# One GNN kernel: on VectorE, x1 of the row tile before goes ahead of the turned unit

## What is computed

```python
h = maximum(layernorm(x), 0)
support = relu(quantised(h) @ quantised(weight))        # small integers
x1 = x + adj @ quantised(support)                       # layer 0
h = maximum(layernorm(x1), 0)
A = (adj + adj.T) * 0.5 + I ;  d = rowsum(A) ** -0.5    # layer 1
y = adj @ ((d[:, None] * A * d[None, :]) @ h)
out = x1 + y
```

## Time and profile before

| what | value |
|---|---|
| median of 3 runs | 499.73 us (499.46 to 500.01) |
| profiled execution, its own time | 499.41 us |
| its span | 497.5 us |
| TensorE (PE) matmul busy | 482.9 us, 97% |
| VectorE (DVE) busy | 275.2 us, 55% |
| ScalarE (ACT) busy | 136.0 us, 27% |
| GpSimd (POOL) busy | 46.5 us, 9% |
| granted TensorE clock | full in all 40 slices |

### The profile page before, as it was taken

The page is one execution under the profiler, slowest core; times in us unless marked ns, Lnnn a source line. Parts: engine busy times, 40 slices in busy tenths (PEclk is TensorE's granted clock), DMA queues, the critical chain, the costliest instruction groups (busy, mean ns, idle before and its releaser), DMA issues.

```text
span 497.5 us, 6362 instructions
## 1 busy us (share of the span) xinstructions
PE 482.9 (97%) x2390; PEld 236.6 (48%) x2390; DVE 275.2 (55%) x367; ACT 136.0 (27%) x192; POOL 46.5 (9%) x54
## 2 busy tenths in 40 slices
PE   3999998999999999999999999999999999999997
PEld 2755554445554444444444444444444444444446
DVE  6964969989999688785996777340000000000000
ACT  1796634433432343534512122140000000000000
POOL 2322932332200000000000000000000000000000
PEclk9999999999999999999999999999999999999999
DMA  8978996779677233233223231045010000100001
GB/s 296 402 315 191 303 243 130 130 172 208 152 216 288 65 106 124 87 107 104 86 89 122 88 123 42 1 134 224 22 42 21 21 21 21 42 21 21 22 21 43
DMA packets 54731, 60.56 MB, mean 122 GB/s; under 512 B 37688, under 2 KB 37944, under 8 KB 54712
## 3 DMA queue, kind: packets, MB, share of 16 engines
q1 hardware_dynamic: 54704, 60.30, 40.5%
q10 hardware_dynamic: 8, 0.00, 0.0%
HBM read 42.99 MB, written 8.39 MB: 103 GB/s over the span
## 4 chain that ended last, share of the span: by engine, by line
PE 84%; DVE 7%; DMA 3%; SPq 2%; ACT 1%; issue 1%; POOL 0%; ACTq 0%; DVEq 0%; POOLq 0%
PE ps_a L1163 31%; PE ps_p L1062 13%; PE ps_p L1126 7%; PE ps_a L1126 7%; PE ps_b L1126 7%; PE ps_m L1126 4%; PE ps_h L1126 4%; DMA feat<-in_x 2%; DVE at L720 2%; PE ps_b L1013 1%; PE ps_m L1062 1%; PE ps_h L1062 1%; DVE at L715 1%; DVE small L900 1%; PE ps_b L1179 1%
## 5 line engine op out<-in xcount | busy, mean ns | idle before, releaser
L1062 PE MATMUL ps_p<-small,at 128*128 128x512 f16 x448 | 100.0, 379 | 2.0 <-DVE feat L840 2.0
L982 DVE SCALAR_TENSOR_TENSOR feat<-ps_a,feat 128x512 f32<-128x512 f32 (+1 forms) x16 | 10.8, 676 | 148.7 <-PE ps_a L1163 144.2
L1163 PE MATMUL ps_a<-small,at 128*128 128x512 f16 x360 | 80.2, 379 | 0.0
L1163 PE MATMUL ps_a<-a_in,at 128*128 128x512 f16 x360 | 80.2, 379 | 0.0
L1062 PEld LDWEIGHTS ps_p<-small,at 128*128 128x128 f16 x448 | 43.6, 98 | 51.5 <-DVE feat L840 2.5
L551 ACT ACTIVATE split<-a_in 128x1024 f16<-128x1024 f32 x30 | 31.7, 1057 | 101.5 <-PE ps_p L1126 90.0
L1163 PEld LDWEIGHTS ps_a<-a_in,at 128*128 (+1 forms) x360 | 35.2, 98 | 42.5
L1163 PEld LDWEIGHTS ps_a<-small,at 128*128 (+1 forms) x360 | 35.2, 98 | 42.5
L896 DVE TENSOR_TENSOR split<-a_in,split 128x1024 f16<-128x1024 f32 x30 | 36.7, 1224 | 33.7 <-ACT split L551 33.7
L1126 PE MATMUL ps_p<-feat,split 128*128 (+1 forms) x180 | 43.9, 379 | 0.5 <-DVE small L900 0.5
L1126 PE MATMUL ps_a<-feat,split 128*128 (+1 forms) x180 | 43.8, 379 | 0.0
(11 more groups left out here) (179 smaller groups left out, 432.5 us busy)
## 6 DMA issues: line engine op xcount, KB each, us to landing
a_in<-in_adj SPq DMA_DIRECT2D x46, 512.0 KB, 3.9
at<-in_adj SPq DMA_DIRECT2D x16, 512.0 KB, 10.0
out<-feat SPq DMA_DIRECT2D x31, 256.0 KB, 4.2
feat<-in_x SPq DMA_DIRECT2D x8, 512.0 KB, 10.8
feat<-out SPq DMA_DIRECT2D x4, 1024.0 KB, 9.3
at<-in_L_gnn_weight SPq DMA_DIRECT2D x2, 512.0 KB, 3.8
at<-at SPq DMA_TRANSPOSE x34, 3.3
split<-in_adj SPq DMA_DIRECT2D x1, 512.0 KB, 16.2
```

The costliest lines, as they stand in the source:

```text
L982: nc.vector.scalar_tensor_tensor(out, products, 1.0 / (SA * SZ), out, ALU.mult, ALU.add).then_inc(y_out, 1)
L1062: last = nc.tensor.matmul(l0_bank(r), at_block(r, lo, j), small[:, j * D:(j + 1) * D], start=(j == 0 and lo == 0), stop=(j == T - 1 and lo ...
L1163: last = nc.tensor.matmul(BANK[n], at_block(t, lo, j), z_part(j, z_lo), start=(j == 0 and lo + z_lo == 0), stop=(j == T - 1 and lo == 1))
```

## The change

VectorE does `x1_tile(r - 1)` before the turned unit of row tile r instead of after it, for every r from 1 to 13. No instruction is added, taken away or changed; TensorE, ScalarE, GpSimd and SP keep their order.

```diff
             for r in range(1, 14):
                 now = TURNS[r]
+                x1_tile(r - 1)
                 for u in now[:1]:
                     turned_out(u)
-                x1_tile(r - 1)
                 moves = MOVES.get(r, [])
                 for u in moves[:1]:
                     lo_rows(u)
```

## The result

The changed kernel takes **502.41 us** (median of 12 runs) against 499.67 us for the kernel before, run beside it (median of 12). The ratio is 1.0050, with a 95% interval of 1.0036 to 1.0064: slower by 1.8 to 3.2 us. One of the twelve runs took 859.19 us at a mean granted clock of 0.66 and is left out of the ratio; without it the median is 502.39 us. The prediction was 502.3 us. The profiled execution took 503.11 us with a span of 501.2 us, 3.7 us more than the span before. Of that, 0.45 us lies ahead of all that the change touches: a turn that TensorE begins at 41.59 before begins at 42.04 here, ahead of the first x1 that was moved. It is still 0.45 us at POOL's sum of unit 17, which starts at 77.80 here and at 77.35 before; this is the last point at which the two profiles run alike.

The account below looks back on a forecast made before the run. TensorE was taken to bound the kernel, with one 2.14 us stall to give back. 2.14 gained against 4.74 us of new stalls made net +2.6 on 499.73: 502.3 us, range 500.1 to 503.8.

Parts of the forecast that it names:

- stall at 77: TensorE's wait between row tiles 4 and 5 for VectorE's x1 of tile 3; it goes, gaining 2.14 us.
- meeting 1: POOL's sum of unit 19 starts 0.64 us before VectorE reaches L720 of unit 17; VectorE becomes 1.62 us late.
- meeting 2: POOL's sum of unit 21 starts 0.57 us before VectorE's L720 of unit 19; VectorE becomes 2.19 us late.
- meeting 3: POOL's sum of unit 23 starts 0.26 us before VectorE's L720 of unit 21; VectorE becomes 3.97 us late.
- turn of unit 24: The reload behind VectorE's late L720 of unit 23 lands at 116.8; TensorE stands about 3.5 us.
- The swap at x1 of tile 7: x1 comes first at 105.63, so TensorE may have row tile 9 at 106.43, when it wants it; nothing lost.
- in stalls at units 24, 28 and 30 together: TensorE's waits for late reloads at these three units, 4.74 us of new stalls, leave it 2.6 us behind.
- 1.4 behind: After its wait for the reload of unit 24, TensorE is 1.4 us behind the kernel before.
- Nothing for r = 1 to 3: In these row tiles the swap moves VectorE's work by up to 2 us but meets long ScalarE waits: no effect.
- Rival A: VectorE does both L720 before POOL's sum at 84.26, so the gain stays: 497.6 us; chance 0.10 with its softer form.
- Its softer form: Only the second meeting of POOL's sum with VectorE's L720 is missed: 498.5 us; chance 0.10 together with Rival A.
- Rival B: POOL's late sums of units 25 or 29 fall where VectorE reads PSUM; it regains about 2.0 us: 500.3; chance 0.10.

## Why the prediction was right

Taken by its own steps, in the clock of before (after, less 0.45 us):

| step | predicted | measured |
|---|---|---|
| stall at 77 | gone, 2.14 gained | gone, 2.14 |
| POOL's sums of 19, 21, 23 | 84.26, 92.04, 98.95 | 84.26, 92.04, 98.94 |
| after meeting 1: x1 of tile 5 | 88.74 | 88.76 |
| after meeting 2: L708 | 95.41 | 95.39 |
| after meeting 3: L708 | 103.43 | 103.44 |
| L720 of unit 23, late by | 2.70 | 2.67 |
| turn of unit 24, wait before it | about 3.5 | 3.71 (3.54 of it idle in the profile) |
| L720 of unit 29, late by | 2.70 | 2.61 |
| layer 1, late by | 2.6 | 3.27 (profile), 2.7 (medians) |

- *POOL's sums move with TensorE and VectorE stands for the rest of each.* Right, and shown from both sides: by moving POOL alone and by moving TensorE alone.
- *VectorE meets the sums again and again.* Right; the margins were to be 0.64, 0.57 and 0.26 us and were 0.34, 0.56 and 0.25, as VectorE came 0.3 earlier to the first. The first meeting is no chance of one execution: in all six profiles of kernels that have it, VectorE came second, by 0.25 to 0.76 us.
- *Late once, late to the end.* Right: L720 of unit 29 starts at 135.34 against 132.73. The blocks at L887 stayed, since the reload of unit 25 landed late as well, as the prediction had it: the sum of 25 came at 111.35, when near 110.7 was expected.
- *The swap at x1 of tile 7 costs nothing.* Right, and more than that: without it TensorE waits 2.1 us there. The end is not later for it (87.64 us in the table against 88.11), since less was left to wait for at unit 24 and the clock stayed full in that profile.
- *"in stalls at units 24, 28 and 30 together"*: this is the step that failed, though the total was nearly right. There was no wait at 28 and 30. After the one at 24 TensorE ran at half the clock for a while and lost 1.73 us, so it came to units 28 and 30 after their reloads had landed. The sum had 3.5 us at unit 24 and 1.2 at the two others; the profile has 3.71 and 1.73, and 5.41 in all (2.14 gained and 3.27 late). The reload of unit 30 landed where the sum has the turn of unit 30, at 142.2 in the clock of before (139.66 and 2.6 are 142.26); the turn came at 143.00, 0.7 us later, and this is what the total was short by for the profiled execution. TensorE's full clock after its waits was taken for granted: the kernel before had only the one of 2 us in this stage, and a longer one was forecast without asking what it does to the clock.
- *502.3 against 502.41.* The mechanism earned the direction and the size, but not the last tenth: the medians give 2.7 us of loss where the profile gives 3.27. So close a hit is in part luck.
- *"1.4 behind"* at unit 24 is a slip by its own terms: 116.8 less 115.48 is 1.3. Measured were 1.57 us, as the reload took 4.96 us in place of 4.8.
- *Nothing for r = 1 to 3.* Right in the sum: VectorE ran elsewhere (an L720 of 3.21 us at 62.58), and was at unit 13 again at 72.08 against 72.38.
- Rival A (497.6) needed VectorE at unit 17 more than 0.64 us earlier; it came 0.30 earlier. It is what the kernel is once POOL's sums are out of the way. Its softer form, the second meeting missed, at 498.5, was run as such: 498.7. Rival B, that a later block dissolves, did not come: VectorE's two L887 took 3.25 and 3.27 us (3.26 and 3.27 before).

## What to carry to other kernels

When a stall of the engine that paces the others is removed, whatever it releases starts earlier too: before counting the gain, put those starts against the other engines' instructions, here POOL's sums against VectorE's instructions with two inputs in SBUF. An engine that is nearly full can't take back what it has lost (VectorE was 2.67 us late at unit 23 and still 2.61 at unit 29), and a chain of buffers hands it to the bottleneck; one wait that puts the sum behind the instruction it would hold up was worth 5 us here, and it is that wait which turns the change from a loss of 0.5% into a gain of 0.4%. Judge such a change by a length between two marks in the profile (83.02 and 83.05 us in the two profiles of one kernel), since whole runs of one kernel differ by 1.4 us and more.

## What the runs showed that had not been expected

- A wait of 3.54 us cost TensorE half its clock for about 3.5 us behind it, 1.73 us of work; waits of 2.1, 1.9, 1.3 and 1.0 us in the profiles of the other kernels left the granted clock at 1.00. This is not the whole of it: of the kernel before, nine of 90 runs beside the experiments had a mean clock of 0.996 or 0.997 too, at 500.90 to 502.49 us. Where in these runs it fell is not on record.
- A VectorE instruction of 128x128 elements with both inputs in SBUF (L891, 0.29 us, where POOL is not in its way) took 2.32 us in the kernel with the sum of 19 later, until 0.15 us after the sum of 25 had ended there (110.67 and 110.52), so smallness did not protect it.
